# First mixture of experts routed and dispatched batch by batch, with scattered rows instead of gathered ones

## Chip, cores and metric

One core of one Trainium2 chip runs the whole program. The metric is the device time of one execution in microseconds; the figure for the kernel before is the median of three runs, 1198.72 us.

## The reference

Two transformer layers run on x of shape (2, 1024, 256), float32. Each layer computes `x = x + ga * attention(h)` and `x = x + gb * ffn(h)`, where h is a LayerNorm scaled and shifted by six vectors made from a condition. Only the first layer's mixture of experts is touched:

```python
logits = x @ gate_w.T                      # 2048 tokens, 64 experts
topv, topi = jax.lax.top_k(logits, 8)
rw = softmax(topv)
gu = einsum('nh,eih->nei', x, gu_w)        # gate and up, 64 wide each
inter = silu(gate) * up * W[:, :, None]    # W: rw at the chosen experts, else 0
out = einsum('nei,ehi->nh', inter, dp_w) + sigmoid(x @ sh_gate1_w.T) * shared(x)
```

## The kernel before, in words

Tokens lie 128 to a tile: tiles 0 to 7 are batch 0, tiles 8 to 15 batch 1. One block of the program (lines 916 to 1556) holds the first layer's attention, the routing, the experts and their combination. All five engines have an order written out by hand there, and they meet at a barrier before and after it.

**Block before it** (L650 to L827). LayerNorm and the q, k, v projections. SP loads inputs, then waits for the modulation rows, stores them to DRAM (L675) and reads them back to all partitions (L678).

**Attention.** For tile t, PE issues `scores(t + 1)`, `values(t - 1)`, `transposes(t)`; DVE takes the maximum (L1329), adds the result of tile t - 2 to x (`output`, L1284 to L1287) and evicts the transposed probabilities; ACT does the exponential. `statistics(g)` and `rows(g)` make the second LayerNorm for a group of four tiles; the rows go to `xn` and to DRAM (`store_rows`, L927).

**Routing.** After the attention: `turned(g)` transposes a group, `logits(g)` multiplies by the gate (L1018), `choose(g)` (L1308) takes the eight largest and a mask. Matrix multiplies by triangular constants count, for each (token, expert) pair, its slot in a list sorted by expert, where each expert's part is rounded up to 128 slots. Then 128 pairs of one-hot matrices per direction (L1386, L1225, L1530) and matmuls (L1107) turn the slots into a list of token numbers (`idxg`).

**Units.** There are 191 tiles of slots at most, thus 96 units of two tiles (`UNITS0`). For each unit POOL gathers two times 128 rows (L1539), PE transposes them (`turn`, L1118), ACT evicts (L1261) and stages gate and up weights (L1258), PE multiplies (`gate_up`, L1130), ACT does silu (L1267), DVE the product (L1435) and the staging of the down weights (L1430), PE `down` (L1143), DVE evicts 128x512 to `ys` (L1444), and SP stores that to `expert_rows` (L945). In units 7 to 70 DVE also computes two routing weights per unit (`weight`, L1413).

**Tail.** POOL gathers, for each of 16 token tiles, its 8 rows (L1551); two buffers, so tile t waits for the sum of tile t - 2. PE, ACT do the shared expert (L1037, L1236). DVE adds the eight weighted rows (`combine`, L1458 to L1461), and makes the second layer's modulation (`conditioned`, `guarded`) and its first LayerNorm groups on the way. The second layer starts after a barrier.

## Time and profile before

| | us |
|---|---|
| median of 3 runs (1197.88 to 1201.56) | 1198.72 |
| the profiled execution | 1203.47 |
| its span, first to last instruction | 1201.7 |
| PE busy / DVE busy / ACT busy / POOL busy | 907.1 / 869.8 / 567.8 / 520.3 |
| first layer's attention, from the block's start | 61.9 to 143.5 |
| routing, to POOL's first gather of a unit | 143.5 to 206.7 |
| 96 units | 214.0 to 458.9 |
| tail, to the second layer's first instruction | 458.9 to 639.6 |
| second layer | 639.6 to 1201.7 |

The stages follow each other; an engine's total over the whole span therefore says little, and a stage is read by itself. The mean granted TensorE clock is 0.895 of 2.4 GHz.

### The profile page before, as it was taken

The page shows a single profiled execution, that of the slowest core. Times are in us where ns is not written, and L with a number is a line of the kernel's source. Part 1 is how long each engine was busy: PE and PEld are TensorE (multiplying, and loading weights), DVE is VectorE, ACT ScalarE, POOL GpSimd, SP SyncE. Part 2 cuts the span into 40 slices and gives each one's busy share as a digit, 9 for nine tenths or more (in the row PEclk, how much of TensorE's full clock was granted, in tenths as well). Part 3 has the DMA queues.
Part 4 walks back from the last instruction along what each step waited for, and adds up shares of the span by engine and source line. Part 5 has one row for each costly group of instructions (what it writes and reads, how often), then busy time and mean ns, then how long its engine had stood idle before and what let it go on. Part 6 is the DMA issues. An engine that isn't in the chain of part 4 may idle for free. (4 is left out here: it accounts for less than half of the span.)

```text
span 1201.7 us, 16894 instructions
## 1 busy us (share of the span) xinstructions
PE 907.1 (75%) x5172; PEld 581.4 (48%) x5172; DVE 869.8 (72%) x2535; ACT 567.8 (47%) x1243; POOL 520.3 (43%) x532
## 2 busy tenths in 40 slices
PE   6899976888888884000007989999988899999887
PEld 5766744666666663000004433333322467688565
DVE  6467887599989873566445888878887569777465
ACT  3322267566666662000004366777768543434553
POOL 3100048777777764777774431111112144453000
PEclk9989985899999997555557999999999999999899
DMA  5060161677767765333332622222211300110001
GB/s 160 1 278 19 38 158 26 187 212 209 211 205 211 220 206 180 103 98 97 103 94 87 214 84 72 72 72 72 72 19 27 118 27 28 52 53 1 1 27 45
DMA packets 74522, 124.97 MB, mean 104 GB/s; under 512 B 12282, under 2 KB 52288, under 8 KB 73024
## 3 DMA queue, kind: packets, MB, share of 16 engines
q1 hardware_dynamic: 58944, 81.80, 22.3%
q0 software_dynamic: 15360, 41.96, 12.5%
q8 instruction: 42, 0.69, 0.2%
q14 instruction: 48, 0.39, 0.1%
q10 hardware_dynamic: 128, 0.13, 0.1%
HBM read 83.80 MB, written 35.66 MB: 99 GB/s over the span
## 5 line engine op out<-in xcount | busy, mean ns | idle before, releaser
L2026 DVE CUSTOM_DVE_ANT_0 masked<-ps,causal 128x128 f32<-128x128 f32 (+7 forms) x256 | 181.1, 755 | 40.7 <-PE ps L1825 39.7
L1539 POOL DMA_INDIRECT h_t<-modulated_rows,ga_rows x192 | 182.8, 952 | 60.8 <-issue 55.2
L145 PE MATMUL ps<-consts,xn 128*128 128x128 f32 x128 | 20.1, 308 | 177.1 <-PEq L78 104.2
L1551 POOL DMA_INDIRECT big<-expert_rows,slot x128 | 126.0, 984 | 55.2 <-issue 40.5
L2006 ACT ACTIVATE xn<-ps 128x512 f32<-128x512 f32 (+3 forms) x256 | 111.7, 511 | 43.6 <-PE ps L1847 42.7
L1458 DVE SCALAR_TENSOR_TENSOR xn<-big,weights,xn 128x256 f32<-128x256 f32 x128 | 62.5, 488 | 84.4 <-DMA big<-expert_rows,slot 80.4
L151 ACT ACTIVATE h_t<-ps,modc 128x512 f32<-128x512 f32 x24 | 17.4, 778 | 192.3 <-PE ps L145 97.9
L1130 PE MATMUL ps<-h_t,xn 128*128 128x128 f32 x768 | 104.9, 281 | 0.0
L145 PEld LDWEIGHTS ps<-consts,xn 128*128 128x128 f32 x128 | 16.8, 160 | 182.0 <-issue 109.9
L1130 PEld LDWEIGHTS ps<-h_t,xn 128*128 128x128 f32 x768 | 96.5, 197 | 0.9 <-issue 0.9
L1118 PE MATMUL ps<-consts,h_t 128*128 128x128 f32 x384 | 64.5, 292 | 35.9 <-DMA h_t<-modulated_rows,ga_rows 35.5
L1847 PE MATMUL ps<-qk 99*128 99x512 bf16 (+3 forms) x288 | 86.6, 333 | 5.4 <-ACT xn L2006 3.1
L1261 ACT COPY h_t<-ps 128x512 f32<-128x512 f32 x96 | 56.3, 586 | 61.0 <-PE ps L1118 59.6
L1825 PE MATMUL ps<-qk 96*128 96x512 bf16 (+3 forms) x288 | 74.6, 327 | 10.8 <-DVE hmax L2026 9.4
L1430 DVE COPY xn<-room 64x256 f32 x192 | 70.4, 366 | 8.4 <-DMA room<-in_down 7.0
L119 POOL TENSOR_TENSOR rstd<-veps,minus_half 128x4 f32<-128x4 f32 x16 | 17.4, 1089 | 135.7 <-DVE veps L130 135.6
L1435 DVE TENSOR_TENSOR rows_b<-rows_b,ps 64x128 f32<-64x128 f32 x192 | 55.8, 291 | 27.9 <-ACT rows_b L1267 24.1
L1118 PEld LDWEIGHTS ps<-consts,h_t 128*128 128x128 f32 x384 | 41.5, 144 | 70.5 <-DMA h_t<-modulated_rows,ga_rows 50.3
L1143 PE MATMUL ps<-xn,rows_b 64*128 64x256 f32 x384 | 68.4, 432 | 3.7 <-issue 3.5
L1444 DVE COPY h_t<-ps 128x512 f32<-128x512 f32 x96 | 66.4, 692 | 5.3 <-DMA expert_rows<-h_t 2.1
L1793 POOL TENSOR_SCALAR_AFFINE_SELECT rzb<-rzb 128x512 f32<-128x512 f32 x24 | 15.6, 651 | 124.3 <-ACT rzb L2006 124.3
L1258 ACT COPY xn<-big 128x256 f32 x192 | 67.6, 400 | 3.6 <-issue 1.2
(321 smaller groups left out, 2184.4 us busy)
## 6 DMA issues: line engine op xcount, KB each, us to landing
expert_rows<-h_t SPq DMA_DIRECT2D x96, 256.0 KB, 2.6
qk<-qk_parts SPq DMA_DIRECT2D x72, 128.0 KB, 2.7
big<-in_gu SPq DMA_DIRECT2D x8, 1024.0 KB, 11.2
qk_parts<-parts SPq DMA_DIRECT2D x16, 384.0 KB, 2.6
raw<-in_mlp SPq DMA_DIRECT2D x16, 384.0 KB, 3.1
room<-in_down SPq DMA_DIRECT2D x4, 1024.0 KB, 10.7
h_t<-modulated_rows,ga_rows POOLq DMA_INDIRECT x192
h_t<-qk_parts SPq DMA_DIRECT2D x24, 128.0 KB, 2.7
```

The costliest lines, as they stand in the source:

```text
L1118: last = nc.tensor.transpose(ps[:, u % 2, (i * KC + c) * P:(i * KC + c + 1) * P], xg[:, u % 4, i, c * P:(c + 1) * P], ident)
L1130: last = nc.tensor.matmul(ps[:, 2 + u % 2, i * P:(i + 1) * P], gus[:, u % 2, i, c * P:(c + 1) * P], hs[:, u % 2, (i * KC + c) * P:(i * KC ...
L1143: last = nc.tensor.matmul(ps[:, 4 + 2 * (u % 2) + i, 0:D], its[i * H:(i + 1) * H, u % 2, :], downs[i * H:(i + 1) * H, u % 2, :], start=Tru ...
L1258: last = nc.scalar.copy(gus[:, u % 2, n, :], big[:, bass.ds(values4[2 * (u % 2) + n], D)])
L1430: last = nc.vector.tensor_copy(downs[n * H:(n + 1) * H, u % 2, :], room[0:H, bass.ds(values4[2 * (u % 2) + n], D)])
L1444: nc.vector.tensor_copy(ys[:, u % 2, :, :], ps[:, 4 + 2 * (u % 2):6 + 2 * (u % 2), 0:D]).then_inc(s_ye, 1)
L1539: nc.gpsimd.indirect_dma_start(xg[:, u % 4, i, :], None, row_dram, bass.IndirectOffsetOnAxis(ap=idxg[:, 2 * u + i:2 * u + i + 1].bitcast(U ...
L1551: nc.gpsimd.indirect_dma_start(yg[:, t % 2, k, :], None, y_dram, bass.IndirectOffsetOnAxis(ap=slots[:, n:n + 1].bitcast(U32), axis=0))\
L1825: last = nc.tensor.matmul(out, qs[v % 3][0:KR, h, i * P:(i + 1) * P], ks[v % 3][0:KR, h, lo:lo + wd], start=True, stop=True)
L1847: last = nc.tensor.matmul(out, ks[v % 3][0:KM, h, j * P:(j + 1) * P], qs[v % 3][0:KM, h, q0 * P:q0 * P + wd], start=True, stop=True)
L2006: nc.scalar.activation(p_tile(at, h)[:, 0:w], ps[:, ST + s % 3, 0:w], ACT.Exp, scale=HD ** -0.5).then_inc(s_exp, 1)
L2026: nc.vector.tensor_tensor_reduce(masked[:, at % 2, 0:k], ps[:, bank:bank + (k + GW - 1) // GW, :] .rearrange("p a n -> p (a n)")[:, 0:k], ...
```

## The change

- Slots are numbered per batch: 64 units for each, 128 in all. Before `down`, a slot's row in DRAM is rearranged so that one partition's two rows lie side by side.
- `row_dram`, the one-hot matrices and the list of token numbers go. POOL instead scatters each token tile's rows (`xn`) to their 8 slots in `dispatched_rows` (`send`), and SP loads a unit's rows with one plain transfer.
- Slots that no token fills must hold something finite: SP fills `dispatched_rows` beforehand, 16 transfers of 1 MB for each batch, the first in the block before the attention (from a tile that POOL sets to zero), the second, from loaded weights, during the attention. The attention block's loads wait for the first fill.
- Batch 0 is routed inside batch 1's attention: PE does `turned` and `logits` for groups 0 and 1 after tiles 8 to 11, does not run `scores(12)` and `scores(13)` ahead, and makes the ranks at tile 12; DVE has `statistics`, `rows`, `choose`, `tiled` and `slotted` between tiles.
- POOL sends batch 0 in order (with the LayerNorm step of groups 2 and 3 after tiles 0 and 3), then batch 1; it makes the shared expert's product after that.
- ACT takes one half of each eviction to `ys`; DVE keeps the other. DVE's weights lie at steps 1 to 64.
- When batch 0's 64 units are stored, POOL fetches its rows back while batch 1's units run, and DVE adds them from step 72, three of a tile's ten steps in every two units. Its shared expert is done between batch 1's units. The tail holds batch 1's eight tiles alone; the second layer's last modulation steps follow its last two tiles.

The diff, cut to what the prediction speaks of:

```diff
-SLOTS = (T * TOPK + E0 * (P - 1)) // P
-UNITS0 = (SLOTS + 1) // 2
+SLOTS = (SEQ * TOPK + E0 * (P - 1)) // P
+UB = (SLOTS + 1) // 2
+UNITS0 = BATCH * UB
...
+        sent_dram = nc.dram_tensor("dispatched_rows", (UNITS0 * 2 * P, D), F32, kind="Internal").ap()
...
+            FILLS = UB * 2 * P * D // (P * 2 * P * TOPK)
+            def fill(engine, b, rows_from):
+                rows = sent_dram[b * UB * 2 * P:(b + 1) * UB * 2 * P, :].rearrange("(n p r) d -> n p (r d)", n=FILLS, p=P)
+                for n in range(FILLS):
+                    engine.dma_start(rows[n], rows_from).then_inc(s_void[b], 16)
...
+                    sp.wait_ge(s_clean, 1)
+                    fill(sp, 0, nothing[:, :])
...
+                    nc.gpsimd.memset(nothing[:, :], 0.0).then_inc(s_clean, 1)
...
+            shared_at = {UB + 2 + 20 * t // 3: t for t in range(TB)}
...
+                    sp.wait_ge(s_void[0], 16 * FILLS)
...
+                    fill(sp, 1, big[:, 0:2 * P * TOPK])
...
+                    for i in range(UNITS0 + 7):
+                        if i < UNITS0:
+                            if i % UB == 0:
+                                all_sent(sp, i // UB)
+                            if i == 0:
+                                sp.wait_ge(s_shs, NG)
+                            if i >= 4:
+                                sp.wait_ge(s_t, i - 3)
+                            sp.dma_start(xg[:, i % 4, :, :],
+                                         sent_dram[i * 2 * P:(i + 1) * 2 * P, :].rearrange("(p i) d -> p i d", i=2))\
+                                .then_inc(s_xg[i % 4], 16)
+                        u = i - 7
+                        if u >= 0:
+                            sp.wait_ge(s_ye, u + 1)
+                            sp.wait_ge(s_yea, u + 1)
+                            sp.dma_start(y_dram[u * 2 * P:(u + 1) * 2 * P, :].rearrange("(p i) d -> p i d", i=2),
+                                         ys[:, u % 2, :, :]).then_inc(s_yst[u % 2], 16)
...
                     for t in range(NT):
-                        if t + 1 < NT:
+                        if t + 1 < NT and t not in (11, 12):
                             scores(t + 1)
                         if t:
                             values(t - 1)
                         transposes(t)
-                    turned(0)
+                        if t in (8, 10):
+                            turned((t - 8) // 2)
+                        if t in (9, 11):
+                            logits((t - 9) // 2)
+                        if t == 11:
+                            scores(12)
+                        if t == 12:
+                            pe.wait_ge(s_cst, 2)
+                            count(0)
+                            pe.wait_ge(s_q, 1)
+                            ranks(0, ps[:, 3, :].rearrange("p (t e) -> p t e", t=TB), 0, TB)
+                            pe.wait_ge(s_key, 1)
+                            scores(13)
...
+                        u = i - 3
+                        if u >= 0:
+                            act.wait_ge(s_d, u + 1)
+                            if u >= 2:
+                                act.wait_ge(s_yst[u % 2], 16 * (u // 2))
+                            nc.scalar.copy(ys[:, u % 2, 1, :], ps[:, 5 + 2 * (u % 2), 0:D]).then_inc(s_yea, 1)
+                            if u in shared_at:
+                                shared_out(shared_at[u])
...
+                    def tiled(b):
+                        dve.wait_ge(s_cnt, b + 1)
+                        counted = ps[0:E0, 5 if b else 3, 0:1]
+                        link(nc.vector.tensor_scalar(q_i[:, b:b + 1], counted, float(P - 1), None, ALU.add))
+                        link(nc.vector.tensor_scalar(q_i[:, b:b + 1], q_i[:, b:b + 1], 7, None, ALU.logical_shift_right))
+                        nc.vector.tensor_copy(q16[:, b, :], q_i[:, b:b + 1].to_broadcast([H, P])).then_inc(s_q, 1)
+                    def slotted(b):
+                        dve.wait_ge(s_exd, 2 * b + 2)
+                        dve.wait_ge(s_rank, b + 1)
+                        nc.vector.tensor_tensor(key[:, b * TB:(b + 1) * TB, :],
+                                                ps[:, 4 if b else 3, :].rearrange("p (t e) -> p t e", t=TB),
+                                                m16[:, b * TB:(b + 1) * TB, :], ALU.mult).then_inc(s_key, 1)
+                        dve.wait_ge(s_key, b + 1)
+                        for t in range(b * TB, (b + 1) * TB):
+                            last = nc.vector.max(pos[:, t, :], key[:, t, :])
+                        link(last)
+                        to = slots[:, b * TB * TOPK:(b + 1) * TB * TOPK]
+                        at = pos[:, b * TB:(b + 1) * TB, :].rearrange("p t k -> p (t k)")
+                        start = float(b * UB * 2 * P - 1)
+                        link(nc.vector.tensor_scalar(to, at, start, None, ALU.add))
+                        nc.vector.tensor_scalar(in_unit[:, 0, :], to, 2 * P - 1, None, ALU.bitwise_and)
+                        link(nc.vector.tensor_scalar(in_unit[:, 1, :], to, P, None, ALU.bitwise_and))
+                        nc.vector.tensor_copy(moved[:, 0, :], in_unit[:, 0, :])
+                        link(nc.vector.tensor_scalar(moved[:, 1, :], in_unit[:, 1, :], -(2 * P - 1) / P, None, ALU.mult))
+                        link(nc.vector.scalar_tensor_tensor(moved[:, 0, :], at, start, moved[:, 0, :], ALU.add, ALU.add))
+                        nc.vector.scalar_tensor_tensor(to, moved[:, 1, :], 0.0, moved[:, 0, :], ALU.add,
+                                                       ALU.add).then_inc(s_slot, 1)
...
+                        if t in (6, 9, 14):
+                            statistics((6, 9, 14).index(t))
+                        if t in (7, 10, 16):
+                            rows((7, 10, 16).index(t))
+                        if t in (10, 12):
+                            choose((10, 12).index(t))
+                        if t == 12:
+                            tiled(0)
+                            slotted(0)
...
-                    for t in range(2, NT):
-                        one_hot_tiles(t)
...
+                    def combine_part(n):
+                        t, j = divmod(n, PARTS)
+                        rows_in = returned(t)
+                        total = rows_in[:, 0, :]
+                        if j == 0:
+                            dve.wait_ge(s_yg[t % 2], 16 * TOPK * (t // 2 + 1))
+                            dve.wait_ge(s_she, t + 1)
+                            link(nc.vector.scalar_tensor_tensor(total, total, w8[:, t, 0:1], sh_out[:, t % 2, :],
+                                                                ALU.mult, ALU.add))
+                        elif j < TOPK:
+                            link(nc.vector.scalar_tensor_tensor(total, rows_in[:, j, :], w8[:, t, j:j + 1], total,
+                                                                ALU.mult, ALU.add))
+                        elif j == TOPK:
+                            link(nc.vector.tensor_tensor(total, total, rows_b[:, 2, t // TB, :], ALU.mult))
+                        else:
+                            nc.vector.tensor_tensor(x_tok[:, t, :], x_tok[:, t, :], total, ALU.add).then_inc(s_ac, 1)
...
-                            nc.vector.tensor_copy(ys[:, u % 2, :, :],
-                                                  ps[:, 4 + 2 * (u % 2):6 + 2 * (u % 2), 0:D]).then_inc(s_ye, 1)
-                        if 8 <= i < 8 + NT * TOPK // 2:
-                            for n in range(2 * (i - 8), 2 * (i - 8) + 2):
+                            nc.vector.tensor_copy(ys[:, u % 2, 0, :], ps[:, 4 + 2 * (u % 2), 0:D]).then_inc(s_ye, 1)
+                        if 1 <= i < 1 + NT * TOPK // 2:
+                            for n in range(2 * (i - 1), 2 * (i - 1) + 2):
                                 weight(n)
...
+                        if i in (UB // 2 + 1, UB + 1):
+                            normalized(i // UB)
+                        late = i - UB - COMBINE_AT
+                        if late >= 0:
+                            for n in range(min(3 * late // 2, TB * PARTS), min(3 * (late + 1) // 2, TB * PARTS)):
+                                combine_part(n)
...
+                    dve.wait_ge(s_ac, TB)
+                    for g in range(GB):
+                        ln_stats(g, link)
+                    for g in range(GB):
+                        ln_rows(dve, g, s_early, 2)
+                    for t in range(TB, NT):
+                        for j in range(PARTS):
+                            combine_part(t * PARTS + j)
+                        if t - TB < 6:
+                            conditioned(t - TB)
+                        else:
+                            guarded(t - TB - 6)
...
+                    def send(t):
+                        if t >= 2:
+                            pool.wait_ge(s_sent[t % 2], SENT * (t // 2))
+                        for n in range(t * TOPK, (t + 1) * TOPK):
+                            nc.gpsimd.indirect_dma_start(
+                                sent_dram, bass.IndirectOffsetOnAxis(ap=slots[:, n:n + 1].bitcast(U32), axis=0),
+                                xn[:, t, :], None).then_inc(s_sent[t % 2], 16)
+                    def fetch(t):
+                        if t >= 2:
+                            pool.wait_ge(s_ac, t - 1)
+                        for k in range(TOPK):
+                            n = t * TOPK + k
+                            nc.gpsimd.indirect_dma_start(
+                                returned(t)[:, k, :], None, y_dram[0:(t // TB + 1) * UB * 2 * P, :],
+                                bass.IndirectOffsetOnAxis(ap=slots[:, n:n + 1].bitcast(U32), axis=0))\
+                                .then_inc(s_yg[t % 2], 16)
+                    for t in range(NT):
+                        if t % TB == 0:
+                            pool.wait_ge(s_slot, t // TB + 1)
+                            pool.wait_ge(s_void[t // TB], 16 * FILLS)
+                        send(t)
+                        if t in (0, 3):
+                            ln_pool(pool, 1, (GB + t // 3,))
+                    all_sent(pool, 1)
...
...
-                    for u in range(UNITS0):
-                        if u >= 4:
-                            pool.wait_ge(s_t, u - 3)
-                        for i in range(2):
-                            nc.gpsimd.indirect_dma_start(
-                                xg[:, u % 4, i, :], None, row_dram,
-                                bass.IndirectOffsetOnAxis(ap=idxg[:, 2 * u + i:2 * u + i + 1].bitcast(U32), axis=0))\
-                                .then_inc(s_xg[u % 4], 16)
...
+                    pool.wait_ge(s_wt, NT * TOPK)
+                    pool.wait_ge(s_gu, UB)
+                    for b in range(BATCH):
+                        for n in range(2):
+                            pool.wait_ge(s_yst[n], 16 * ((b + 1) * UB // 2))
+                        if b:
+                            ln_pool(pool, 2, range(GB))
+                        for t in range(b * TB, (b + 1) * TB):
+                            fetch(t)
```

## Rows read from the trace of the kernel before

**Rows 1.** Busy time by stretch: us and count per engine, granted clock, DMA share, GB/s

```profile
62.00:143.00 81.00, 77.21 (x347) 55.54 (x348) 59.60 (x162) 18.61 (x44) 5.23 (x13) 0.97 0.32 123
143.00:206.00 63.00, 46.29 (x267) 31.84 (x266) 55.75 (x238) 46.68 (x125) 39.66 (x53) 0.70 0.32 77
214.00:459.00 245.00, 212.97 (x1536) 164.78 (x1536) 210.44 (x735) 154.56 (x382) 176.96 (x187) 0.97 0.68 202
474.00:640.00 166.00, 2.40 (x10) 2.04 (x11) 92.76 (x246) 1.45 (x2) 119.25 (x121) 0.50 0.33 95
```

**Rows 2.** Groups by line, units' stretch: count, busy us, mean ns, idle us

```profile
L1539 POOL DMA_INDIRECT h_t<-modulated_rows,ga_rows x187 | 177.7, 951 | 57.0 <-issue 54.0 <-PE ps L1118 3.0
```

**Rows 3.** Timeline of PE's transposes in the units: start us, us

```profile
223.14 0.66 PE L1118 MATMUL ps<-consts,h_t 128*128 128x128 f32 x4
...
225.25 0.66 PE L1118 MATMUL ps<-consts,h_t 128*128 128x128 f32 x4
```

**Rows 4.** Timeline of DVE in one unit with weights, and its last eviction

```profile
262.36 0.59 DVE L1435 TENSOR_TENSOR rows_b<-rows_b,ps 64x128 f32<-64x128 f32 x2
...
262.98 0.69 DVE L1444 COPY h_t<-ps 128x512 f32<-128x512 f32 x1
...
263.59 0.28 DVE L1413 SCALAR_TENSOR_TENSOR weight_scratch<-swap,slot_plus_one 128x64 f32<-128x64 f32 x1
...
264.86 0.60 DVE L1435 TENSOR_TENSOR rows_b<-rows_b,ps 64x128 f32<-64x128 f32 x2
...
457.37 1.50 DVE L1444 COPY h_t<-ps 128x512 f32<-128x512 f32 x2
```

**Rows 5.** Timeline before and after the units: first unit, first fetch, last combine

```profile
213.99 1.94 PE L1118 MATMUL ps<-consts,h_t 128*128 128x128 f32 x8 [8.42 <-DMA h_t<-modulated_rows,ga_rows]
...
462.39 0.94 POOL L1551 DMA_INDIRECT big<-expert_rows,slot  x1 [14.72 <-DMA expert_rows<-h_t]
...
632.87 4.13 DVE L1458 SCALAR_TENSOR_TENSOR xn<-big,weights,xn 128x256 f32<-128x256 f32 x8 [5.19 <-DMA big<-expert_rows,slot]
...
639.56 1.41 DVE L125 BATCH_NORM_STATS2 stats<-x_tok 128x6 f32<-128x256 f32 x4 [1.64 <-PEq L78]
```

**Rows 6.** Groups by line, 474 to 636 us, in the tail

```profile
L1551 POOL DMA_INDIRECT big<-expert_rows,slot x119 | 117.5, 987 | 38.1 <-issue 38.1
```

**Rows 7.** Timeline of the first layer's attention and its LayerNorm

```profile
103.98 0.48 DVE L1284 SCALAR_TENSOR_TENSOR room<-ps,rz,bv 128x256 f32<-128x256 f32 x1 [3.12 <-PE ps L997]
...
112.07 0.82 DVE L1329 TENSOR_REDUCE mx<-ps 128x1 f32<-128x640 f32 x1 [0.67 <-PE ps L970]
...
120.55 1.67 DVE L1300 SCALAR_TENSOR_TENSOR xn<-x_tok,mv,rows_b 128x256 f32<-128x256 f32 x4
```

**Rows 8.** Timeline of the routing after the attention

```profile
142.74 3.69 PE L1018 MATMUL ps<-big,h_t 128*128 128x66 f32 x32
...
151.03 0.60 DVE L1314 MAX8 top<-swap 128x8 f32<-128x64 f32 x4
...
153.25 0.60 DVE L1314 MAX8 top<-swap 128x8 f32<-128x64 f32 x4
...
162.21 1.29 DVE L1365 TENSOR_TENSOR swap<-ps,chosen_mask 128x512 f32<-128x512 f32 x2 [0.48 <-PE ps L1092]
...
163.53 2.12 DVE L1370 MAX8 slot_plus_one<-swap 128x8 f32<-128x64 f32 x16
...
165.96 1.17 DVE L1374 TENSOR_SCALAR slot_part<-slot 128x128 int32<-128x128 int32 x1
```

**Rows 9.** SP's timeline: the broadcast load of the modulation rows

```profile
61.13 0.37 SPq L678 DMA_DIRECT2D rows_b<-modulation_rows  x1
```

**Rows 10.** DMA share and GB/s in short stretches, columns as in Rows 1

```profile
17.00:20.00 3.00, 2.76 (x13) 1.92 (x11) 2.61 (x2) 0.00 (x0) 2.72 (x2) 1.00 0.09 36
70.00:75.00 5.00, 5.00 (x25) 3.68 (x25) 3.67 (x10) 1.13 (x3) 0.00 (x0) 1.00 1.01 428
99.00:100.00 1.00, 0.52 (x4) 0.16 (x2) 0.97 (x3) 0.22 (x1) 0.00 (x0) 1.00 1.02 348
```

397 lines of the change are left out of this document (150 added, 247 removed).

## The prediction

> **What bounds the kernel now.** I read the stretches first. They follow each other with barriers or full waits between them, so the change can only pay in the four of [rows 1]. In the attention (62 to 143 us) PE is busy 77.2 of 81 us: what is put there lengthens it. From 143 to 206 us no engine is full and the clock falls to 0.70; that is the routing, a chain. In the units (245 us) PE has 213 and DVE 210 us, but the group of POOL's gathers [rows 2] shows who sets the pace: 177.7 busy and 57.0 between issues make 234.7 us for 187 gathers, 1.255 us each, two per unit, 2.51 us. PE by itself needs less: where rows are ready, its transposes are 2.11 us apart [rows 3]. In the tail only POOL is full: (117.5 + 38.1) / 119 = 1.31 us per fetch [rows 6], 128 of them.
>
> So POOL issues 192 + 128 indirect transfers now, all on the path: 241 + 168 us. After the change there are 128 sends and 128 fetches, and of these only the first 64 sends (up to the first unit) and the last 64 fetches stand alone. Against that stand 32 more units.
>
> **The sum.** Stage by stage, against the profiled execution (1203.47 us); the median of the runs is 4.75 us below it, and I take the difference over to it. About 0.3% (3.6 us) is what a measurement of this kernel can tell from no change.
>
> *Block before the attention, +1.* The loads at the start are over at about 17.3 us: from 17 to 20 us the DMA engines are busy 9% [rows 10]. Then 16 MB of zeros are written (16.78 MB) until SP stores the modulation rows, whose read back goes out at 61.13 us [rows 9]; the block's barrier waits for it. The store stands behind the fill. The trace has no store with rows of 8 KB: loads with such rows run at 428 GB/s, a store with rows of 1 KB at 348 [rows 10]. That makes 39.2 or 48.2 us, an end at 56.5 or 65.5, so 0 or +5.5 us. I take +1, near the load, since it has the same row size. The Trainium skill gives a lower ceiling; it is a rival below. The zeroing itself (POOL, idle then) and the second fill (from about 82 us, beside an idle DMA) I cost at nothing; the second is needed only at the second batch's sends.
>
> *Attention until batch 0's slots.* The maximum of tile 12 is taken at 112.07 us [rows 7]. Between tiles 9 and 12 DVE now also has statistics 2.0 (1.41 [rows 5] and two short steps), `rows` 2 x 1.67 [rows 7] and one `choose`, 2.2 from one to the next [rows 8]: 7.6 us. PE no longer runs `scores(12)` ahead, so behind DVE's copy come values, transposes, logits (1.85, half of the 3.69 in [rows 8]) and scores, some 5 us in the open. Tile 12's maximum moves to about 125. From there: its own maximum, output and eviction 3.1, `choose` 2.2, counting 0.5, ranks on PE 1.6, the product 0.65 (half of 1.29), eight MAX8 1.06, and the slots' arithmetic about 2.4, two of whose steps are integer ANDs of 64 columns at half of 1.17 [rows 8]. This is 11.5 us: 136.6. PE stands idle in these waits for the first time, and where it did so after the attention the granted clock was 0.70 [rows 1]; I add 2: slots at 139.
>
> *To the first unit, +13.* 64 sends. No scatter is in the trace; its nearest row is the gather of the same 128 rows of 1 KB, 1.255 us: 80.3 us, with 2.6 for two LayerNorm steps, 0.7 to start, 1.5 to land, 3 for SP's load. First transposes at 227 us, against 213.99 [rows 5]. Batch 1's routing ends before that: `rows(3)` has to wait for POOL, which makes rstd of group 3 after four tiles of sends (about 180), and from there to the expert numbers I count 24 us, 204. It is hidden by 18 us of sends; the one-hot loop (some 35 us) is gone altogether.
>
> *Units, +63.* DVE, in the stretch where it also makes weights: product 0.62, eviction 0.61, weights and the next staging 1.27, together 2.50 us a unit [rows 4], with no idle. It is as full as POOL. It gives up half of the eviction (0.27): 2.23 in batch 0's units. ACT was busy 154.6 us in 96 units [rows 1], 1.61 each; its half eviction, 0.4, makes 2.0. PE stays at 2.11. So DVE sets the pace; I take 2.27 for 64 units, 145.3. In steps 65 to 71 DVE has neither weights nor sums, PE's 2.15 counts: 8 x 2.15 = 17.2. The first fetch can only start when unit 63 is stored and takes 8 x 1.31 + 2.8; DVE reaches its first sum about 2 us before. From step 72 on DVE has 1.5 sums per unit at 4.13 / 8 = 0.516 each [rows 5], 0.76: staging 0.70, product 0.62, half eviction 0.34, sums 0.76 = 2.42, taken as 2.44 for 54 units, 131.8. Then 2 units and the drain, 8, a cold start of 2, and 2 for crowded DMA. In all 145.3 + 17.2 + 2 + 131.8 + 12 = 308 us. Before, from 213.99 to the last eviction at 458.87 [rows 4, 5], it was 245.
>
> *DMA in the units.* Load and store of a unit are 524 KB in 2.27 us, 231 GB/s; batch 1's sends, for 80 us beside them, 104: 335 GB/s. The old gathers and stores moved 202 GB/s at a share of 0.68, the fetches alone 95 at 0.33, that is 297 and 288 at a full share [rows 1]. Rows of 2 KB should lie between 348 and 428: 231/390 + 104/288 = 0.95. It just fits, hence the 2 us.
>
> *Tail, -80.* After the last unit DVE makes statistics for two groups (4.1) and POOL their rstd before its first fetch: 5.4 us. Then 63 fetches of 1.32, 2.8 to land, the last sum 5.05, now `guarded` (1.0) and ACT's first modulation (1.45) behind it, barrier 1.64: 100.6 us. Before it was 639.56 - 458.87 = 180.7.
>
> Sum: +1 + 13 + 63 - 80 = **-3 us**: 1196 us. The second layer is unchanged. A gain of 80 us in the tail and of all the one-hot work pays almost exactly for 32 units of 2.4 us.
>
> **Bounds.** Fill 0 to +5.5. Slots of batch 0: the waits could overlap better or worse, -5 to +6. A send could be cheaper than a gather, since nothing has to come back, but its issue is what counts: -1 to +4. The units carry most: at PE's 2.11 and 2.30 under the sums they take 18 us less, at the 2.51 of before 17 us more. Tail -3 to +3.
>
> **The rivals.**
>
> *Units at the engines' own limits (faster), 1180 us.* For it: DVE's groups of 2.50 us include overlaps that shrink when an eviction is halved, and 2.11 was reached as soon as rows were there [rows 3]. Against it: sums are linked one to the next.
>
> *The pace stays at 2.51 (slower), 1213 us.* The eviction is now on two engines, in ACT's order between staging and the hidden rows' copy. PE's `down(u + 2)` and SP's store wait for both halves; ACT at 2.0, PE at 2.11 and DVE at 2.23 leave 0.1 to 0.3 us for every semaphore of the ring. If ACT's half comes late, SP stores late, and DVE, the fullest engine, waits for its buffer (it did so 2.1 us in all before). Place: each `ys` eviction. Price: 128 x (2.51 - 2.38) = 17 us. It decides early: a mean pace above 2.43, only 0.05 over mine, makes the kernel slower by over 0.3%.
>
> *DMA saturates while batch 1 is sent (slower), 1211 us.* If 2 KB rows run no better than the 290 to 297 of [rows 1], sends leave 185 GB/s: 2.83 us per unit, 28 units instead of 35 in 80 us, +16 us. It starts where the engines' ceiling is below 335. For it: nothing in the trace ran two such streams; against it: 428 GB/s seen. The Trainium skill (DMA: Bandwidth & Descriptors, Issuing engines are not separate DMA queues) says that transfers of all issuing engines run on the same 16 engines and interleave; by that rule SP's loads get no way round POOL's sends, and no run here shows it yet.
>
> *A send costs more than a gather (slower), 1211 us.* At 1.5 us each, 64 on the path are +16; the other 64 are hidden.
>
> *The fill ends late (no change), 1200 us.* The modulation rows' store stands behind it in SP's queue and holds up the barrier of all engines; at the 348 GB/s of the only store in [rows 10] +5.5, thus 4.5 over my sum. The Trainium skill (DMA: Bandwidth & Descriptors, Specifications) puts a core's HBM limit at about 358 GB/s; by it the fill would take an estimated 47 us and end at 64, +4. The trace disagrees for loads, with 428.
>
> **How the numbers follow.** The forecast, 1196 with its own range of 1188 to 1204, has 0.37. Faster rival 0.25; pace unchanged 0.13; DMA 0.09; dear sends 0.08; fill 0.08. Faster by over 0.3% (below 1195.1): 0.25 and 0.17 of the forecast's, 0.42. Slower (above 1202.3): 0.30 and 0.04, 0.34. The rest, 0.24, is no change. Range 1178 to 1218: it takes in all rivals; beyond are two together.
>
> **What would show it.** Right: first `turn` at 222 to 232 us, behind the 64th send; POOL's sends 1.25 us apart; 2.2 to 2.35 us per unit in batch 0 and 2.4 to 2.5 under the sums; the second layer starting at about 636 us; last eviction to there 100 us. Wrong: the attention's first instruction after 63 us (fill), PE waiting for `xg` at a DMA share near 1 (saturation), DVE or ACT waiting for each other's half with none of them full (pace), the first unit waiting for the expert numbers (routing, not sends), or a sum waiting for fetched rows in every tile.

## The result, and the profile after

The changed kernel takes **1221.85 us** (median of 4 runs, 1221.35 to 1223.6), the kernel before 1200.09 beside it: ratio 1.0186, 95% interval [1.0163, 1.0208]. It is slower, and lies outside the range of 1178 to 1218. The profiled execution took 1223.6 us with a span of 1221.9; all times below are its own, unless a run is named. Against the span before (1201.7) it is 20.2 us longer, where the sum said 3 us shorter: 23.2 us to find.

Busy time by stage after the change (the view by windows, columns as in [rows 1]). The stages are: attention, routing and sends of batch 0, units of batch 0, eight units without sums, units with sums, tail.

```profile
62.00:168.50 106.50, 91.17 (x401) 64.62 (x401) 68.02 (x210) 21.87 (x52) 23.22 (x28) 0.90 0.64 259
168.50:235.80 67.30, 19.28 (x77) 11.91 (x77) 15.71 (x74) 10.03 (x21) 47.53 (x51) 0.63 0.61 178
235.80:390.70 154.90, 145.67 (x1044) 113.91 (x1044) 128.53 (x577) 115.08 (x324) 64.06 (x65) 0.96 0.85 275
390.70:409.50 18.80, 17.69 (x130) 13.76 (x130) 12.84 (x45) 14.55 (x43) 10.61 (x12) 1.00 0.88 280
409.50:556.20 146.70, 122.93 (x893) 95.05 (x891) 123.25 (x362) 103.51 (x283) 54.81 (x53) 1.00 0.77 243
556.20:655.80 99.60, 6.94 (x24) 5.15 (x24) 54.20 (x165) 5.75 (x11) 64.88 (x66) 0.51 0.38 115
```

The units (235.8 to 556.2 us) last 320.5 us, where [rows 1] has 245 and the sum had 308. PE is busy for 94, 94 and 84% of its three stretches and DVE for 83, 68 and 84: no engine is shown as full, so each stretch has to be read for its own waits. Landing means the time from a transfer's issue until its semaphore says that it has arrived; a linked step is one that waits for the result of the step before it.

**To the first unit.** POOL and PE (timeline, all rows that waited for something but the issue before):

```profile
141.73 1.22 POOL L1583 DMA_INDIRECT dispatched_rows<-xn,slot  x1 [32.46 <-DVE slot L1400]
...
153.32 1.04 POOL L120 TENSOR_TENSOR rstd<-veps,minus_half 128x4 f32<-128x4 f32 x1 [1.51 <-DVE veps L131]
...
191.16 1.04 POOL L1583 DMA_INDIRECT dispatched_rows<-xn,slot  x1 [5.12 <-DMA dispatched_rows<-xn,slot]
...
235.78 1.98 PE L1156 MATMUL ps<-consts,h_t 128*128 128x128 f32 x8 [26.69 <-DMA h_t<-dispatched_rows]
```

The third row is new: after 32 sends, before those of tile 4, POOL stands still until tile 2's rows have landed, since `send(t)` waits for tile t - 2 on a shared semaphore. (Two expectations below call this place tile 5, counting from one.) What was in the way is in the DMA issues from 168 to 192 us (engine, count, KB each, median us to landing), beside 15 sends:

```profile
room<-in_down SPq DMA_DIRECT2D x4, 1024.0 KB, 14.7
```

and in the share of the DMA engines (the part of the time that the 16 of them were busy), 1.02 between 170 and 190 us, for this load and the sends together (windows):

```profile
170.00:190.00 20.00, 5.06 (x21) 2.80 (x21) 6.13 (x28) 0.38 (x1) 12.55 (x13) 0.74 1.02 243
```

The first transposes stand at 235.78 us, 21.8 behind [rows 5].

**Batch 0's units.** SP's store of a unit and ACT's evictions behind it (timeline):

```profile
271.11 0.32 SPq L981 DMA_DIRECT2D expert_rows<-h_t  x1
...
272.86 0.37 ACT L1301 COPY h_t<-ps 128x256 f32<-128x256 f32 x1 [0.62 <-DMA expert_rows<-h_t]
...
275.46 0.37 ACT L1301 COPY h_t<-ps 128x256 f32<-128x256 f32 x1 [0.88 <-DMA expert_rows<-h_t]
```

There are two store buffers, used in turn (the ring of two), so a unit's eviction waits for the store of two units before. The store issued at 271.11 has its buffer free at 275.46: 4.35 us. One took 6.3: issued at 300.53, and ACT and DVE both stand until 306.8. The view of waits from 240 to 560 us gives the sum of it (us, times, longest):

```profile
ACT h_t L1301 <- DMA expert_rows<-h_t: 50.9, 62, 3.2
...
DVE h_t L1518 <- DMA expert_rows<-h_t: 15.9, 21, 2.8
```

Of the evictions of ACT between 238 and 316 us some 20, well over half, waited for a landing, with a median of about 4.1 us from the store's issue (of these stores alone, so of the slower ones). The DMA engines carry this in the same time (windows):

```profile
250.00:310.00 60.00, 55.76 (x408) 42.50 (x407) 51.20 (x231) 44.45 (x128) 42.80 (x45) 1.00 0.96 323
```

From the first silu (239.72) to that of unit 64 (390.67) it is 2.36 us a unit.

One gap in it has another cause. Once POOL has made its last send, it multiplies the shared expert's gate and up parts, and while it does so DVE's copies of the down weights take over four times as long as just before (timeline):

```profile
319.59 0.58 DVE L1504 COPY xn<-room 64x256 f32 x2
...
320.68 4.99 POOL L1609 TENSOR_TENSOR room<-room 64x512 f32<-64x512 f32 x4 [3.74 <-issue]
...
323.19 2.63 DVE L1504 COPY xn<-room 64x256 f32 x2
```

From the silu at 324.03 to the next at 330.33 it is 6.3 us in place of 2.1: this product costs batch 0 about 4.2 us. In e6_nosend, below, POOL makes it from 231.59 us on, ahead of the units, and the silus of the same two units (316.18, 318.64) are 2.46 us apart. In all other runs the product stands within batch 0's units too.

**Under the sums.** A unit and a half of DVE's (timeline), with the register load in the gap:

```profile
435.99 0.42 DVE L1518 COPY h_t<-ps 128x256 f32<-128x256 f32 x1
436.33 0.47 DVE L1482 SCALAR_TENSOR_TENSOR swap<-swap,weights 128x256 f32<-128x256 f32 x1
437.32 0.72 DVE L1504 COPY xn<-room 64x256 f32 x2 [0.52 <-DVE swap L1482]
438.07 0.59 DVE L1509 TENSOR_TENSOR rows_b<-rows_b,ps 64x128 f32<-64x128 f32 x2
438.70 0.42 DVE L1518 COPY h_t<-ps 128x256 f32<-128x256 f32 x1
439.04 0.47 DVE L1482 SCALAR_TENSOR_TENSOR swap<-swap,weights 128x256 f32<-128x256 f32 x1
```

Such a gap of 0.52 us stands ahead of the staging in 23 of the 27 pairs of units between 409 and 553 us. Behind a sum with no register load after it the timeline still has 0.13 us (440.16 after 439.04 and 0.99), so the register load itself costs 0.39 us a pair. From 318 to 390 us, in batch 0's units, where no linked sum stands ahead of the same register load, the gaps before the staging are 0.2 us in all. Silu to silu it is 2.61 us a unit, from 409.48 to 553.31.

**The tail** is 99.6 us (last row of the first fence), as forecast (100.6). **The second layer**, not touched, is 3.9 us longer: from the barrier to the end 562.1 before and 566.05 after. Both kernels' first projection, and the first scores after it, from the timelines; before:

```profile
641.30 7.98 PE L1887 MATMUL ps<-h_t,swap 128*128 128x512 f32 x16
...
665.34 0.33 PE L1825 MATMUL ps<-qk 96*128 96x128 bf16 x2 [0.54 <-ACT v_ones L1978]
```

and after:

```profile
657.59 8.74 PE L1951 MATMUL ps<-h_t,swap 128*128 128x512 f32 x16
...
684.32 0.33 PE L1889 MATMUL ps<-qk 96*128 96x128 bf16 x2 [2.47 <-DMA qk<-qk_parts]
```

PE's clock rises 0.8 us later, and 2.5 us are waited for a transfer, after which the clock is 0.64 from 683.8 to 687.8 us. All of it falls in the layer's first 32 us. In the profiles of the twelve experiments the layer took 562.7 to 568.0 us, so part of this is spread, but none was as short as the one profile of before. Why the transfer lands later stays open.

### The profile page after: what moved, and what is told of

Same layout as the page of the kernel before. It is cut to its first block and busy times, and to the rows that moved or that the text cites. A ratio compares the mean times of both kernels' runs of the same rounds, so it can differ in the third digit from the quotient of the medians.

```text
span 1221.9 us, 18659 instructions
## 1 busy us (share of the span) xinstructions
PE 967.3 (79%) x5549; PEld 626.7 (51%) x5549; DVE 852.7 (70%) x2580; ACT 609.3 (50%) x1403; POOL 431.1 (35%) x417
## 5 line engine op out<-in xcount | busy, mean ns | idle before, releaser
L1583 POOL DMA_INDIRECT dispatched_rows<-xn,slot x128 | 124.4, 972 | 79.7 <-issue 41.8
L1168 PE MATMUL ps<-h_t,xn 128*128 128x128 f32 x1024 | 138.9, 280 | 5.3 <-issue 5.2
L1168 PEld LDWEIGHTS ps<-h_t,xn 128*128 128x128 f32 x1024 | 127.3, 196 | 7.5 <-issue 7.3
L1184 PE MATMUL ps<-xn,rows_b 64*128 64x256 f32 x512 | 90.8, 428 | 28.0 <-issue 20.7
L1294 ACT COPY xn<-big 128x256 f32 x256 | 90.2, 402 | 28.9 <-DMA dispatched_rows<-xn,slot 25.0
L1301 ACT COPY h_t<-ps 128x256 f32<-128x256 f32 x128 | 47.5, 371 | 60.9 <-DMA expert_rows<-h_t 50.9
L1593 POOL DMA_INDIRECT big<-expert_rows,slot x64 | 62.6, 978 | 21.2 <-issue 21.2
L1593 POOL DMA_INDIRECT xn<-expert_rows,slot x32 | 32.7, 1022 | 104.1 <-DMA expert_rows<-h_t 69.9
L1518 DVE COPY h_t<-ps 128x256 f32<-128x256 f32 x128 | 54.3, 425 | 20.5 <-DMA expert_rows<-h_t 15.9
L1911 PEld LDWEIGHTS ps<-qk 99*128 99x128 bf16 x288 | 25.9, 97 | 76.3 <-ACT xn L2070 42.5
```

The lines of the kernel that those rows point to most:

```text
L1168: last = nc.tensor.matmul(ps[:, 2 + u % 2, i * P:(i + 1) * P], staged_gu(u, i)[:, c * P:(c + 1) * P], hs[:, u % 2, (i * KC + c) * P:(i * K ...
L1184: last = nc.tensor.matmul(ps[:, 4 + 2 * (u % 2) + i, 0:D], its[i * H:(i + 1) * H, u % 2, :], staged_down(u)[i * H:(i + 1) * H, :], start=T ...
L1294: last = nc.scalar.copy(staged_gu(u, n), big[:, bass.ds(values4[2 * (u % 2) + n], D)])
L1583: nc.gpsimd.indirect_dma_start(sent_dram, bass.IndirectOffsetOnAxis(ap=slots[:, n:n + 1].bitcast(U32), axis=0), xn[:, t, :], None).then_in ...
L1593: nc.gpsimd.indirect_dma_start(returned(t)[:, k, :], None, y_dram[0:(t // TB + 1) * UB * 2 * P, :], bass.IndirectOffsetOnAxis(ap=slots[:, ...
L1911: last = nc.tensor.matmul(out, ks[v % 3][0:KM, h, j * P:(j + 1) * P], qs[v % 3][0:KM, h, q0 * P:q0 * P + wd], start=True, stop=True)
```

## The experiments

All are edits to the changed kernel. Paces are from silu to silu in the profile: units 0 to 64, 72 to 127 ("under sums"), and 74 to 127 ("from 74").

| run | median us | ratio to before | first transposes | batch 0 | under sums | from 74 |
|---|---|---|---|---|---|---|
| changed | 1221.85 | 1.0186 | 235.78 | 2.36 | 2.61 | 2.61 |
| e1_sems4 | 1217.16 | 1.0143 [1.0127, 1.0160] | 231.19 | 2.28 | 2.62 | 2.60 |
| e2_ys3 | 1216.38 | 1.0140 [1.0121, 1.0158] | 238.04 | 2.17 | 2.68 | 2.57 |
| e3_regs | 1213.39 | 1.0117 [1.0099, 1.0135] | 233.28 | 2.30 | 2.48 | 2.43 |
| e4_act | 1212.09 | 1.0123 [1.0100, 1.0146] | 236.82 | 2.28 | 2.43 | 2.38 |
| e5_nosum | 1207.84 (one) | - | 235.87 | 2.33 | 2.35 | 2.33 |
| e6_nosend | 1212.49 (one) | - | 234.18 | 2.18 | 2.62 | 2.61 |
| e8_route_after | 1243.18 | 1.0355 [1.0335, 1.0374] | 251.65 | 2.36 | 2.64 | 2.58 |
| e9_all | 1188.13 | 0.9900 [0.9879, 0.9920] | 233.34 | 2.19 | 2.28 | 2.17 |
| e10_alt | 1192.84 | 0.9937 [0.9919, 0.9954] | 232.54 | 2.19 | 2.38 | 2.27 |
| e12_pool | 1191.86 | 0.9937 [0.9925, 0.9949] | 228.33 | 2.19 | 2.32 | 2.21 |
| e13_p1 | 1187.65 | 0.9903 [0.9888, 0.9917] | 229.76 | 2.16 | 2.29 | 2.18 |
| e14_nosum_ys3 | 1195.75 (one) | - | 238.54 | 2.20 | 2.28 | 2.17 |

The last two columns differ because of one gap. With three store buffers (e2_ys3 and e9_all to e14_nosum_ys3) DVE reaches the first weighted sum before POOL's first eight fetches have landed, and waits 3.8 to 4.5 us, in the changed kernel 0.5; in e9_all (timeline):

```profile
398.51 0.48 DVE L1489 SCALAR_TENSOR_TENSOR xn<-xn,weights 128x256 f32<-128x256 f32 x1 [4.05 <-DMA xn<-expert_rows,slot]
```

The silus of units 73 and 74 are 7.7 to 8.9 us apart there, 5.4 us or more over the pace: faster units meet a sum that stands at a fixed step. No run moves that step.

Batch 0's first send came between 139.9 and 144.5 us in kernels with the same attention; a stage read from one profile has this spread.

### Sends on four semaphores (e1_sems4)

```diff
-s_sent = [sem(f"c_sent{n}") for n in range(2)]
+s_sent = [sem(f"c_sent{n}") for n in range(4)]
-if t >= 2: pool.wait_ge(s_sent[t % 2], SENT * (t // 2))
+if t >= 4: pool.wait_ge(s_sent[t % 4], SENT * (t // 4))
```

> Edit: the sends of the tiles are counted on four semaphores in place of two, so that a tile's sends wait for the landing of the tile four before, not two before. In the profile of the changed kernel POOL stood 5.12 us before tile 5 at this wait (at 191 us), while the down weights were loaded. Theory A (the wait is the semaphore's, the sends could be issued): the wait is gone, the first transposes of the units come at 230.5 us in place of 235.8, the time falls by 5 us to about 1217. Rival B (the 16 DMA engines are behind, so POOL has to stand still in any case, or the rows land no earlier): the first transposes stay within 1 us of 235.8, and so does the time within 1.5 us.

Theory A. POOL's wait is gone, the first send stands at 141.68 as before, and PE starts 4.6 us earlier:

```profile
231.19 2.21 PE L1156 MATMUL ps<-consts,h_t 128*128 128x128 f32 x8 [21.90 <-DMA h_t<-dispatched_rows]
```

4.7 us less in the median. The DMA engines were as full (1.02 from 170 to 190 us), yet the sends could be issued ahead and their rows landed while POOL went on; it was the wait on the semaphore that turned a slow landing into lost issue time.

### Three store buffers (e2_ys3)

```diff
-ys[:, u % 2, :, :]).then_inc(s_yst[u % 2], 16)
+rows_out(u)).then_inc(s_yst[u % 3], 16)    # third: ga
-if u >= 2: act.wait_ge(s_yst[u % 2], 16 * (u // 2))
+if u >= 3: act.wait_ge(s_yst[u % 3], 16 * (u // 3))
```

> Edit: three buffers in place of two for the experts' rows on their way out (the third is the attention's gate rows, free by then), and nothing else. In the profile of the changed kernel ACT stood 50.9 us (62 times) and DVE 15.9 us (21 times) before the evictions for a store to land. Theory A (the ring of two: eviction 0.4 us and landing 3.5 to 4 us, thus 4.0 to 4.4 us for two units, is longer than the engines' own pace while batch 1 is sent): batch 0's units fall from 2.36 us to 2.15 to 2.2 each, 10 to 13 us less, and the units under the sums stay at 2.61, since DVE has no idle time there. Time about 1211. Rival B (the DMA engines are full during batch 0, shares of 0.91 to 0.98): PE waits for loaded rows in place of it, under 4 us gained. Rival C (the ring also holds up the units under the sums): these fall too, over 16 us gained in all.

Theory A for the place: batch 0 falls to 2.17 us a unit, where the six profiles with two buffers and the sends have 2.28 to 2.36, so 7 to 12 us. In the whole only 5.5 us came out. In this profile the slots were 1.9 us late, and of what batch 0 gains, DVE loses 4.4 us in its wait for the first fetched rows; from unit 74 on the pace is 2.57 us for 2.61, since DVE is full there. (The expert numbers had to be kept elsewhere in this run and in all others with three buffers.)

### Batch 1's sends left out (e6_nosend)

```diff
-send(t)
+if t < TB: send(t)
```

> Edit: the 64 sends of batch 1 are left out (its slots keep their zeros, so batch 1's expert rows are not computed); two store buffers as in the changed kernel. Theory A (the sends beside batch 0's units lengthen the landing of the stores, and the ring of two buffers turns that into pace): landings fall from about 3.9 us to 3.4, batch 0 from 2.36 to 2.12 to 2.18 us a unit, 12 to 15 us less, time about 1208. Rival B (the ring of two is too short by itself): batch 0 stays above 2.25 us a unit, under 7 us less.

Theory A for the pace, 2.18, with two buffers; the whole is 9.4 us shorter, not 12 to 15. The run doesn't isolate its reason. Batch 0's units are 11.3 us shorter in the profile, but about 4 of these are POOL's product for the shared expert, which comes ahead of the units once POOL has no sends there. Some 7 us are left for the landings: ACT waited 14.1 us in 16 times between 240 and 370 us, against 20.4 in 26 times, DVE about as long in both (11.2 and 11.0 us). So stores land late beside the units' own loads and stores too, and the sends make it more frequent.

### DVE's register load moved (e3_regs), evictions moved to ACT (e4_act)

```diff
 last.then_inc(s_in, 1)                 # the product
+if u % 2 and u + 1 < UNITS0:
+    values4 = numbers(u + 1)           # was ahead of the staging
```

> Edit: DVE reads the expert numbers of a pair of units into its registers right behind the product of the unit before, in place of behind the linked weighted sums. In the profile of the changed kernel DVE has, under the sums, a gap of 0.52 us before the first down-weight staging of every second unit, and no other idle time. Theory A (the gap is the register load that starts only when the last sum has ended, and DVE sets the pace there): 0.52 us x 28 pairs = about 14 us less, 2.35 us a unit in place of 2.61; time about 1207. Rival B (DVE's gap only fills what the ring of two stores leaves): under 5 us gained, and the waits for landings on DVE grow. Rival C (the gap moves with the register load, to before the eviction): no change.

8.5 us less: between A and B. The gap is gone from DVE's waits, and from unit 74 on the pace is 2.43 for 2.61, the 2.44 of the prediction. The idle time ahead of the staging from 412 to 540 us (groups by line, busy us, mean ns, idle us), in the changed kernel and in this run:

```profile
L1504 DVE COPY xn<-room 64x256 f32 x96 | 29.7, 310 | 14.8 <-DVE xn L1482 4.2 <-DVE swap L1482 3.6 <-PE ps L1184 1.1
...
L1508 DVE COPY xn<-room 64x256 f32 x104 | 32.8, 315 | 6.9 <-issue 0.2
```

Theory A counted 0.52 us 28 times. What moving the load can save is 0.39 us in 23 places, 9 us, since 0.13 us stays behind a linked sum in any case; under the sums the profile gained 7 us.

```diff
-nc.scalar.copy(ys[:, u % 2, 1, :], ps[:, 5 + 2 * (u % 2), 0:D])
+nc.scalar.copy(ys[:, u % 2, :, :], ps[:, 4 + 2 * (u % 2):6 + 2 * (u % 2), 0:D])   # u >= 72, DVE none
```

> Edit: from the first weighted sum on (unit 72) ACT evicts both halves of a unit in one copy of 512 columns, and DVE none. DVE is spared 0.34 to 0.42 us a unit, ACT pays some 0.2 us. Theory A (DVE sets the pace under the sums, by the sum of its own work): 2.61 us a unit falls to what ACT needs, staging 0.71, eviction 0.59, hidden rows 0.59, silu 0.38 and the shared expert's rows, about 2.35; 14 us less, time about 1208. Rival B (the ring of stores or PE sets it): under 4 us gained. Rival C (ACT becomes the bound, since its copy waits for PE and for the landing before the hidden rows' copy): slower than 1222.

9.8 us less in the median of six runs that spread from 1207.5 to 1219.0, 2.43 a unit; by the profile the units from 72 to 127 gained 10 us. Theory A in direction. What stands in the way of the last 4 us is probably ACT's wait for landings (16.0 us in 24 times from 412 to 540); this run doesn't separate it.

### The sums left out (e5_nosum), and with three buffers (e14_nosum_ys3)

```diff
 elif j < TOPK:
-    link(nc.vector.scalar_tensor_tensor(...))
+    if t >= TB: link(nc.vector.scalar_tensor_tensor(...))
```

> Edit to the changed kernel: of the ten DVE steps per tile of batch 0 that are made under batch 1's units, the seven linked sums after the first are left out (the rows are still fetched); batch 1's tiles keep theirs. It prices what the bringing back of batch 0 costs the units. Theory A (DVE's own work sets the pace under the sums): 2.61 us a unit falls to 2.15 to 2.2, near PE's 2.11, 22 to 25 us less, time about 1198. Rival B (fetches and the ring of two stores hold the pace too): above 2.35 us a unit, under 14 us less. The last eviction to the second layer stays at 98 to 100 us in both.

At the edge of rival B: 2.345 us and 14.0 us, where it said above 2.35 and under 14. DVE now has room, and meets the next limit at once (waits from 412 to 515 us):

```profile
DVE h_t L1519 <- DMA expert_rows<-h_t: 13.3, 19, 1.4
...
ACT h_t L1301 <- DMA expert_rows<-h_t: 20.9, 28, 1.6
```

> Edit: the seven linked sums per tile of batch 0 left out, as in the run before, and three store buffers in place of two. With two buffers the pace without these sums was 2.345 us a unit and DVE waited 13.3 us for stores to land. Theory A (behind DVE's work the ring of two stores was the next limit): 2.12 to 2.2 us a unit from unit 72 on, batch 0 at 2.17 to 2.19, time about 1188 to 1192. Rival B (the fetches at a DMA share of 0.89 hold the pace, whatever the buffers): above 2.3 us a unit under the sums.

The mean of 2.28 lies between both, but it holds the one gap of 8.2 us at the first sum. From unit 74 on it is 2.17, theory A, and the waits for stores are 1.3 us on each engine from 412 to 515 us. The time is above theory A's, 1195.75, with this gap and a start of the units 2.8 us later. The windows from 412 to 515 us, of the changed kernel:

```profile
412.00:515.00 103.00, 87.24 (x635) 67.95 (x636) 87.30 (x255) 73.04 (x200) 44.80 (x44) 1.00 0.82 256
```

of e5_nosum:

```profile
412.00:515.00 103.00, 97.58 (x709) 75.06 (x707) 75.23 (x235) 77.28 (x221) 49.77 (x51) 1.00 0.89 284
```

and of e14_nosum_ys3:

```profile
412.00:515.00 103.00, 102.48 (x769) 80.82 (x769) 81.21 (x258) 88.61 (x244) 46.47 (x48) 1.00 0.94 302
```

The first count is PE's matmuls, 16 for a unit and a few for the shared expert, a measure of units done: 635, 709, 769. In the last PE is busy throughout (102.48 of 103 us), at a DMA share of 0.94. The fetches beside it cost PE nothing that shows: the silus are 2.11 us apart, as in [rows 3], and 2.5 to 2.6 in every sixth or seventh unit, where PE also does a tile of the shared expert; together 2.17. So three limits lie close together under the sums: DVE at 2.61, the ring of two stores at 2.33, PE at 2.17.

### Batch 0 routed behind the attention (e8_route_after)

```diff
-if t in (8, 10): turned(...)   # and logits, count, ranks within tiles 8 to 12
+values(NT - 1); turned(0); logits(0); turned(1); logits(1); count(0); ranks(0)
```

> Edit: batch 0 is routed behind the attention in place of within batch 1's tiles (transposes, logits, choice, counting, ranks and slots moved behind the last tile's output; LayerNorm of group 2 on POOL now ahead of the sends). All else as in the changed kernel. Theory A (the routing within the attention pays what its place costs): the attention's last output comes at about 146 us in place of 168.5, batch 0's slots at about 165 in place of 141.4, the first transposes 23 us later at 259, the rest the same: time about 1244. Rival B (the waits of PE and the half clock that the routing brings into the attention cost nearly what it saves): first transposes before 245 us, time under 1231.

Theory A; 1243.18 us. The last output of the attention is at 148.5 us in place of 168.5, the slots come 23.6 us later:

```profile
165.28 1.22 POOL L1573 DMA_INDIRECT dispatched_rows<-xn,slot  x1 [31.10 <-DVE slot L1391]
```

The first transposes are only 15.9 us later, not 23: SP issues the down weights' load at 149 us and so ahead of the sends, POOL waited 0.3 us for landings in place of 5.4, and it no longer waited for group 2's statistics. This is the run that ties the wait to that load. Theory A's time is thus met partly by luck: some 5 us more than at the first transposes came in later stages, 1.5 of them under the sums, the rest in the tail and the second layer, and nothing here says why. The routing within the attention is worth 21 us to this kernel.

### All four together (e9_all), and variants

> Edit: the four edits of the first runs together (sends on four semaphores, three buffers for the rows on their way out, DVE's register load behind the product, ACT evicting both halves from unit 72 on). Theory A (three separate limits: POOL's wait before tile 5, the ring of stores in batch 0, DVE's own work under the sums): first transposes 4.6 us earlier; batch 0 at 2.17 us a unit, 12 us; under the sums ACT is the fullest with about 2.3 us a unit (DVE 2.0, PE 2.11), 17 us; together 34 us, time about 1188, under the kernel before. Rival B (they share one slack, or the DMA engines, at a share of 0.8 to 0.98 already, take the place of the ring): batch 0 stays above 2.25 and the sums above 2.45 us a unit, time about 1200.

Theory A's time, on the microsecond: 1188.13, **1.0% under the kernel before**, and batch 0 at 2.19 us. Under the sums the 2.28 is the 2.3 that theory A gave, but not for its reason. ACT isn't the fullest there, PE is: 103.00 of 103 us, at 2.17 us a unit from unit 74 on, and the mean holds the one gap of 8.6 us at the first sum. Its window from 412 to 515 us:

```profile
412.00:515.00 103.00, 103.00 (x774) 80.96 (x773) 89.36 (x261) 97.40 (x245) 46.86 (x48) 1.00 0.94 304
```

The four edits alone gave 4.7, 5.5, 8.5 and 9.8 us, 28.5 in sum; together 33.7. They do not share a slack. That they give more together isn't clear of noise by itself, each figure being uncertain by some 3 us. A reason for it is at hand, though: the third buffer pays from unit 74 on only once DVE is relieved, from 2.33 to 2.17 without the sums (e5_nosum, e14_nosum_ys3) and from 2.61 to 2.57 with them (e2_ys3).

```diff
-whole = range(UB + COMBINE_AT, UNITS0)       # units that ACT evicts by itself
+whole = range(UB + COMBINE_AT, UNITS0, 2)
```

> Edit: as the run with all four, but from unit 72 on ACT evicts both halves only of every second unit, and the halves are shared in the others. By the engines' own work DVE then has about 2.2 us a unit, ACT 2.15, PE 2.11. Theory A (the pace under the sums is that of the fullest engine): 2.25 us a unit, some 3 us less than the run with all four. Rival B (ACT's order, which waits for PE's down product before the hidden rows' copy, sets the pace): the same time within 1.5 us.

Both theories wrong: 4.7 us slower than with all of ACT's evictions. From unit 74 on it is 2.27 us a unit, near theory A's 2.25, but e9_all, with which it is to be compared, has 2.17 there and not 2.28. PE set the pace in that run, so nothing could be gained by relieving ACT, and DVE became the full engine again: 2.2 us of waits in the 118 from 412 to 530 us, with 105 shown as busy and the rest between its instructions.

```diff
-if t in (0, 3): ln_pool(pool, 1, (GB + t // 3,))       # (1) on POOL
+if t in (1, 3): ln_pool(pool, 1, (GB + t // 3,))
+for t in range(TB):                                    # (2) on POOL, ahead of fetch(t + 2)
+    pool.wait_ge(s_summed, t + 1)
+    made(nc.gpsimd.tensor_tensor(total, total, rows_b[:, 2, 0, :], ALU.mult))
+    nc.gpsimd.tensor_tensor(x_tok[:, t, :], x_tok[:, t, :], total, ALU.add).then_inc(s_ac, 1)
```

> Edit: as the run with all four edits, and (1) POOL makes the rstd of group 2 after the sends of tile 1 in place of tile 0, which spares the 1.5 us that it waited for DVE's statistics; (2) of batch 0's tiles under batch 1's units, the multiplication by the gate row and the addition to x are made by POOL in place of DVE, so DVE has 1.25 linked sums a unit in place of 1.5 steps. Theory A (DVE is still the fullest engine under the sums, 2.28 us a unit, and POOL has idle time there): first transposes 1.5 us earlier, 2.28 falls to about 2.16, 6.5 us; time about 1180. Rival B (ACT or the DMA engines hold 2.28): only the 1.5 us. Rival C (POOL's two steps, late behind a fetch, hold up the next fetch or slow DVE down): 1188 or more.

Rival C: 1191.86, 4.2 us over e13_p1, which has (1) alone. The fetches, now behind POOL's two steps, come late: DVE waited 5.7 us for them from 412 to 515 us, in e13_p1 1.9. From unit 74 on that makes 2.21 us a unit for 2.18, some 1.4 us; 2.1 us more lie in batch 0's units, which edit (2) doesn't touch, so the rest of the 4.2 stays unexplained. Theory A had no room: PE, not DVE, set the pace.

> Edit: as the run with all four edits, and only the first of the two further ones: the rstd of group 2 after tile 1's sends. Theory A: the 64th send and the first transposes come 1.5 us earlier, time about 1186.6. Rival B: the attention's end (rows of group 2 need that rstd) comes later and takes batch 1's routing with it, but that is hidden by some 20 us; no change of the time beyond 1.5 us either way.

1187.65 us, the same as e9_all within its uncertainty. The wait for statistics is gone from POOL, but it is too small for these runs.

## Why the prediction was wrong, step by step

From the kernel before to the changed one, in the span: to the first unit +21.8 (sum: +1 and +13), units +75.6 (+63), tail -81.1 (-80), second layer +3.9 (0). The errors are +7.8, +12.6, -1.1 and +3.9: 23.2 us.

- *Block before the attention, right.* The modulation rows' read-back went out at 61.34 us, against 61.13 in [rows 9]: the fill cost 0.2 us. "The fill ends late" is refuted: from 20 to 50 us the zeros went out at 426 GB/s, above both the 348 and the 358 that this rival used, and at the 428 of the loads.
- *Attention until batch 0's slots, right within 2 us.* Tile 12's maximum was at 126.4 (about 125), the first send at 141.73 (slots at 139). The granted clock was 0.65 from 118 to 141.5 us, so the low clock that I added 2 us for was there; what it cost isn't separated.
- *To the first unit, mis-sized.* Sends were 1.266 us apart (1.255 taken from [rows 2]), so "a send costs more than a gather" (1.5 us) is refuted. Missing were POOL's waits, 1.51 us for statistics and 5.12 for landings. I counted every send as issue alone, and did not ask what the semaphore of `send` waits for while 4 MB of down weights load. The Trainium skill (DMA: Bandwidth & Descriptors, Issuing engines are not separate DMA queues) says that transfers of all engines share the 16 DMA engines; I put that rule against the second batch's sends only, and the trace shows it here as well, at a share of 1.02. Batch 1's routing was hidden, as forecast, with the expert numbers at about 210 us in place of 204.
- *Units of batch 0, the wrong engine:* 151 us for 145.3. The step that failed is "DVE sets the pace; I take 2.27". DVE needs less: with three buffers the same units take 139 us, 2.17 each, near PE's 2.11, so the forecast's own term was 6 us too high. Two terms that it put at nothing stand against that. One is the ring of two stores, landing plus eviction, halved: (4.1 + 0.4) / 2 = 2.25 us where the landings are long, 12 us by e2_ys3. The other is POOL's product for the shared expert, about 4 us. PE's 64 x 2.11 = 135 and these two make the 151, within a us or two. In the kernel before a store of this size lands in 2.6 us (median of 96), by which the ring stands at 1.5; I left it out of the sum, and it grew when loads, stores and sends ran together. The Trainium skill (DMA: Bandwidth & Descriptors, Anatomy of one DMA — SWDGE (gpsimd) path) fits a fixed 2.0 us and bytes over 436 GB/s to transfers that GpSimd issues, which makes an estimate of 2.6 us for these bytes; SP's stores in the trace of before agree with it, the changed kernel's waits don't.
- *DMA in the units, right in its number.* 335 GB/s were forecast; from 250 to 310 us it is 323 at a share of 0.96, and 342 to 347 at 1.00 with three buffers (e14_nosum_ys3, e9_all). It fits, but transfers that fit land later. The rival "DMA saturates" had its place right and its mechanism wrong: PE did not wait for loaded rows, evictions waited for stores.
- *Units under the sums, mis-sized:* 2.61 us for 2.44, 9.6 us over 55 units. The terms were right; what was missing is the register load, 0.39 us in most pairs of units, 0.17 us a unit, which shows once a linked sum stands ahead of it; moved, it gives the 2.43 us of e3_regs. "The pace stays at 2.51" named the point where it decides (above 2.43; the measured mean of all units is 2.47), but with two mechanisms of which one, the wait for a buffer, holds in batch 0, and the other, waiting for each other's half, was not seen.
- *Tail, right:* 99.6 for 100.6.
- *Second layer, "unchanged":* 3.9 us more in this profile, from the clock and one transfer at its start; left open.

The forecast thus had the size of the gain right (80 us of fetches) and the price of the extra units 12.6 us too low. It said 3 us faster, the kernel is 22 us slower, and the two steps that failed most are the pace of the units, put down to each engine's own work with no term for the ring of stores, for POOL's product or for the register load, and the sends, with no term for POOL's waits. With the four edits together the kernel comes to 1188, 8 us under what I had forecast.

## What to carry to other kernels

When a sum makes an engine's own work the pace, price each ring of buffers too: (landing + use) / buffers, with the landing as it will be when the transfers run side by side, and not as it is in the emptier kernel. When work is moved into a loop, look at what it stands ahead of: the register load that was free behind independent instructions cost 0.39 us behind a linked one. Look also at what another engine does at the same time: one product on POOL held up a whole ring of units for 4 us. And when several limits lie within 10% of each other, expect single edits to give less than they promise (here 4.7 of 5, 5.5 of 11, 8.5 of 14 and 9.8 of 14 us), and try them together. A mean pace over a stage can hide one gap: read the distances one by one before a limit is named from it.

## What was not expected of the hardware

- A store of 256 KB took 2.6 us to land in the kernel before, and 4.1 us (median of those waited for), 6.3 at the longest, where all transfers together ran at 323 GB/s.
- The load of the down weights to 64 partitions and the sends beside it filled the DMA engines (1.02) at 243 GB/s; POOL stood for 5.1 to 5.9 us before tile 4's sends in all seven profiles with two semaphores and this order.
- Plain stores of zeros with rows of 8 KB went out at 426 GB/s, from 20 to 50 us.
- While POOL multiplied tiles of 64x512, from 320.68 to 325.67 us, two of DVE's copies took 2.63 us in place of 0.58.
- DVE was full with 89% busy and next to no idle time in the view of waits (e10_alt, 412 to 530 us): the rest lies between its instructions, in gaps too short to be listed, such as 0.13 us behind a linked sum.
- 128 scatters of 128 rows of 1 KB cost 1.266 us each at POOL, the same as gathers.
